# The key maximum over all partitions on TensorE instead of GpSimd, with GpSimd's scatters and two weight halves placed anew

## The reference, cut to what matters

```python
def softmax_kernel(data, proj, is_query, eps=0.0001):
    data_dash = jnp.einsum('bhnd,md->bhnm', data * normalizer, proj)
    diag = jnp.sum(data ** 2, axis=-1, keepdims=True) * 0.5 * normalizer ** 2
    if is_query:
        m = jnp.max(data_dash, axis=-1, keepdims=True)
    else:
        m = jnp.max(data_dash, axis=(-2, -1), keepdims=True)
    return ratio * (jnp.exp(data_dash - diag - m) + eps)
```

## Time and profile before

| | us |
|---|---|
| median of 3 runs | 1915.27 (1909.77 to 1923.55) |
| profiled execution, device time | 1906.49 |
| its span | 1904.7 |
| mean granted TensorE clock, share of full | 0.942 |

### The profile page before, as it was taken

The page is one execution under the profiler, slowest core; times in us unless marked ns, Lnnn a source line. Parts: engine busy times, 40 slices in busy tenths (PEclk is TensorE's granted clock), DMA queues, the critical chain, the costliest instruction groups (busy, mean ns, idle before and its releaser), DMA issues.

```text
span 1904.7 us, 19746 instructions
## 1 busy us (share of the span) xinstructions
PE 1707.0 (90%) x7679; PEld 1322.5 (69%) x7679; DVE 1101.8 (58%) x1835; ACT 673.7 (35%) x879; POOL 1000.7 (53%) x546
## 2 busy tenths in 40 slices
PE   6998999999896699999998299999999859999996
PEld 5664567788764456788886178787777747887863
DVE  7597758999875476756327433423433266623275
ACT  3323534332421244243331255655555412221112
POOL 3224561466778667548860456667676480152402
PEclk9999989999999688899999599999999979999988
DMA  8362111455332211122351767787777341121001
GB/s 331 95 207 50 1 1 48 122 111 111 62 78 22 23 1 1 23 67 45 66 160 34 260 204 264 250 275 246 247 270 240 136 122 45 45 89 43 24 1 45
DMA packets 146780, 212.56 MB, mean 112 GB/s; under 512 B 43740, under 2 KB 60352, under 8 KB 145440
## 3 DMA queue, kind: packets, MB, share of 16 engines
q1 hardware_dynamic: 98736, 177.49, 28.6%
q0 software_dynamic: 42832, 18.84, 8.3%
q10 hardware_dynamic: 5120, 14.99, 2.3%
HBM read 187.21 MB, written 30.08 MB: 114 GB/s over the span
## 4 chain that ended last, share of the span: by engine, by line
PE 65%; DVE 14%; POOL 6%; DMA 5%; ACT 5%; issue 4%; SPq 0%; POOLq 0%; DVEq 0%
PE PS L634 17%; PE PS L636 17%; PE PS L635 17%; PE PS L799 5%; PE PS L813 3%; DMA table_c<-edge_add,edge_ix 2%; POOL table_w L2293 2%; POOL table_c L2293 2%; PE PS L790 2%; ACT kd L1308 2%; PE PS L782 2%; DMA table_w<-edge_add,edge_ix 1%; POOL W L2218 1%; DVE h_op L1946 1%; POOL slots_x L2327 1%
## 5 line engine op out<-in xcount | busy, mean ns | idle before, releaser
L2218 POOL TENSOR_TENSOR W<-raw,W 128x2048 fp32r<-128x2048 f32 x40 | 192.4, 4813 | 330.8 <-ACT W L1158 323.6
L2293 POOL DMA_INDIRECT table_w<-edge_add,edge_ix x128 | 208.6, 1630 | 69.8 <-DMA table_w<-edge_add,edge_ix 39.7
L2293 POOL DMA_INDIRECT table_c<-edge_add,edge_ix x128 | 204.6, 1598 | 60.8 <-issue 33.5
L634 PE MATMUL PS<-op_b,W 128*128 128x512 f32 x576 | 225.5, 392 | 3.6 <-DVE op_b L2025 2.6
L635 PE MATMUL PS<-op_b,W 128*128 128x512 f32 x576 | 224.4, 390 | 0.0
L636 PE MATMUL PS<-op_b,W 128*128 128x512 f32 x576 | 224.4, 390 | 0.0
L634 PE MATMUL PS<-W,op_a 128*128 128x512 f32 x480 | 188.2, 392 | 2.9 <-DVE op_a L1755 1.8
L635 PE MATMUL PS<-W,op_a 128*128 128x512 f32 x480 | 187.1, 390 | 0.0
L636 PE MATMUL PS<-W,op_a 128*128 128x512 f32 x480 | 187.0, 390 | 0.0
L2332 POOL TENSOR_TENSOR W<-raw,W 128x2048 fp32r<-128x2048 f32 x30 | 143.5, 4792 | 56.4 <-ACT W L1389 56.4
L1158 ACT ACTIVATE W<-raw 128x2048 fp32r<-128x2048 f32 x40 | 76.5, 1920 | 158.6 <-PE PS L636 103.3
(11 more groups left out here) (419 smaller groups left out, 3824.2 us busy)
## 6 DMA issues: line engine op xcount, KB each, us to landing
raw<-in_L_ffn_w_dram SPq DMA_DIRECT2D x46, 1024.0 KB, 5.7
raw_e<-in_L_ffn_w_dram SPq DMA_DIRECT2D x22, 1024.0 KB, 5.9
raw_v<-in_L_ffn_w_dram SPq DMA_DIRECT2D x22, 1024.0 KB, 5.2
raw<-in_L_mix_W_dram SPq DMA_DIRECT2D x16, 1024.0 KB, 6.7
raw<-table_c SPq DMA_DIRECT2D x10, 1024.0 KB, 5.2
key_row<-key_dram SPq DMA_DIRECT2D x32, 256.0 KB, 4.0
w_row<-in_edge_weight_dram SPq DMA_DIRECT2D x32, 256.0 KB, 4.8
table_w<-zero POOLq DMA_DIRECT2D x4, 1024.0 KB, 7.9
```

The costliest lines, as they stand in the source:

```text
L634: pe.matmul(ps, lhs_hi, rhs_hi, start=start, stop=False)
L2218: pool.tensor_tensor(lo_at, raw[:, r % 2, :], hi_at.bitcast(F32), ALU.subtract).then_inc(lo_done, 1)
L2293: pool.indirect_dma_start(out=tb, out_offset=bass.IndirectOffsetOnAxis(ap=edge_ix[:, i, c:c + 1].bitcast(U32), axis=0), in_=edge_add[:, i, ...
```

## The change

The eight all-reduces on GpSimd go. TensorE turns `kmaxp` (128 x 2) into 2 x 128 by a transpose after the second query job (job `kt`), VectorE reduces it to `kneg` and multiplies a 2 x 2 unit matrix with it (`kdiag`), TensorE spreads it over 128 partitions by a product with ones after the fourth query job (job `kb`), and VectorE copies that to `nkmax`. ScalarE exponentiates two query tiles ahead of the keys. The column of ones in `V` is written once in place of eight times. GpSimd's scatters no longer stand between all-reduces: in layer 0, ten are put ahead of wo's low half and ten ahead of up's, and each of these two low halves waits for `kdiag_ready` of its pair; four more follow. In layer 1, 13 stand after wv, then wo, 12, up, 12 and 12. The totals (24 and 59 by the end of each attention part, with those of the query and key stage) stay the same.

```diff
--- before.py
+++ after.py
@@ -111,7 +111,8 @@
                    (f"v{l}", 1, "D"), (f"rk{l}", 2, "A"), (f"v{l}", 1, "D"), (f"dk{l}", 1, "A"), (f"v{l}", 6, "D"), (f"vsum{l}", 1, "A")]
         for hp in range(HEADS // 2):
             s = f"{l}.{hp}"
-            stages += [("kd" + s, 8, "AD"), ("qd" + s, 8, "A"), ("ctx" + s, 1, "D"), ("eT" + s, 8, "D"),
+            stages += [("kd" + s, 8, "AD"), ("qd" + s, 2, "A"), ("kt" + s, 1, "D"), ("qd" + s, 2, "A"),
+                       ("kb" + s, 1, "D"), ("qd" + s, 4, "A"), ("ctx" + s, 1, "D"), ("eT" + s, 8, "D"),
                        ("o" + s, 4, "D")]
         stages += [(f"wo{l}", 6, "D"), (f"y2_T{l}", 4, "AD"), (f"wo{l}", 2, "D"),
                    (f"up{l}.0", 2, "A"), (f"y2_T{l}", 4, "AD"), (f"up{l}.0", 6, "A"), (f"down{l}.0", 8, "D")]
@@ -332,7 +333,9 @@
         dexp = place("dexp", [P, 2, NT, HEADS])
         vsum = place("vsum", [P, HEADS, VW])
         kmax = place("kmax", [P, 2, NT])
-        kmaxp = place("kmaxp", [P, 2, 2])
+        kmaxp = place("kmaxp", [P, 2])
+        kneg = place("kneg", [2, 1])
+        kdiag = place("kdiag", [2, 2])
         nkmax = place("nkmax", [P, 2])
         nqmax = place("nqmax", [P, NT, 2])
         ctx_sb = place("ctx_sb", [P, 2, 4, DH])
@@ -439,8 +442,7 @@
         proj_loaded = sem("proj_loaded")
         vsum_ready = sem("vsum_ready")
         kmax_ready = sem("kmax_ready")
-        kmax_all = sem("kmax_all")
-        nkmax_ready = sem("nkmax_ready")
+        kdiag_ready = sem("kdiag_ready")
         kexp_done = sem("kexp_done")
         wg_ready = sem("wg_ready")
         chosen_ready = sem("chosen_ready")
@@ -777,10 +779,20 @@
                     s = f"{l}.{hp}"
                     for x, feat in (("kd", k_T), ("qd", q_T)):
                         for t in range(NT):
-                            n = JOB[x + s] + t
+                            n = JOB_AT[x + s, t]
                             open_job(n)
                             pe.matmul(bank(n), feat[:, hp, t * P:(t + 1) * P], proj[:, :, :].rearrange("p a m -> p (a m)"),
                                       start=True, stop=True).then_inc(job_full, 1)
+                            if x == "qd" and t == 1:
+                                n = JOB["kt" + s]
+                                open_job(n)
+                                pe.wait_ge(kmax_ready, 4 * l + hp + 1)
+                                pe.transpose(bank(n)[0:2, 0:P], kmaxp[:, :], ident[:, :]).then_inc(job_full, 1)
+                            if x == "qd" and t == 3:
+                                n = JOB["kb" + s]
+                                open_job(n)
+                                pe.wait_ge(kdiag_ready, 4 * l + hp + 1)
+                                pe.matmul(bank(n)[:, 0:2], ones[0:2, :], kdiag[:, :], start=True, stop=True).then_inc(job_full, 1)
 
                     def turn(t):
                         n = JOB_AT["eT" + s, t]
@@ -1297,16 +1309,18 @@
                             o_to_hi(hp - 1)
 
                     def query_exp(t):
-                        n = JOB["qd" + s] + t
+                        n = JOB_AT["qd" + s, t]
                         act.wait_ge(qbias_ready, NT * (4 * l + hp) + t + 1)
                         for h in range(2):
                             ins = act.activation(G[:, t, h * NBF:(h + 1) * NBF], bank(n)[:, h * NBF:(h + 1) * NBF], ACT.Exp, bias=nqmax[:, t, h:h + 1])
                         ins.then_inc(job_act, 1)
 
-                    act.wait_ge(nkmax_ready, 4 * l + hp + 1)
+                    for t in range(2):
+                        query_exp(t)
+                    act.wait_ge(job_done, DONES[JOB["kb" + s]])
                     for h in range(2):
                         act.activation(kd[:, h, :, :], kd[:, h, :, :], ACT.Exp, bias=nkmax[:, h:h + 1]).then_inc(kexp_done, 1)
-                    for t in range(NT):
+                    for t in range(2, NT):
                         query_exp(t)
                 o_to_hi(HEADS // 2 - 1)
                 split_hi(f"down{l}.0")
@@ -1669,6 +1683,7 @@
                     dve.wait_ge(job_full, n + 1)
                     if t == 0:
                         dve.wait_ge(job_act, ACTS[JOB[f"dk{l}"]])
+                        dve.tensor_copy(V[:, :, :, DH], dexp[:, 1, :, :])
                     link(dve.tensor_tensor(G[:, t, :], bank(n), rowv[:, row_at[f"bv{l}"] % 3, :], ALU.add))
                     if t:
                         ins = dve.tensor_tensor(v_sum[:, :], G[:, 0, :] if t == 1 else v_sum[:, :], G[:, t, :], ALU.add)
@@ -1677,8 +1692,7 @@
                         else:
                             ins.then_inc(vsum_ready, 1)
                     dve.tensor_tensor(V[:, t, :, 0:DH], G[:, t, :].rearrange("p (h d) -> p h d", h=HEADS),
-                                      dexp[:, 1, t, :].unsqueeze(2).to_broadcast([P, HEADS, DH]), ALU.mult)
-                    dve.tensor_copy(V[:, t, :, DH], dexp[:, 1, t, :]).then_inc(job_done, 1)
+                                      dexp[:, 1, t, :].unsqueeze(2).to_broadcast([P, HEADS, DH]), ALU.mult).then_inc(job_done, 1)
 
                 def o_to_lo(hp, c):
 
@@ -1697,16 +1711,23 @@
                         for c in range(2):
                             o_to_lo(hp - 1, c)
                     dve.wait_ge(job_done, DONES[JOB["kd" + s] + 7])
-                    dve.tensor_reduce(kmaxp[:, 0, :], kmax[:, :, :], AX_X, ALU.max).then_inc(kmax_ready, 1)
+                    dve.tensor_reduce(kmaxp[:, :], kmax[:, :, :], AX_X, ALU.max).then_inc(kmax_ready, 1)
                     for t in range(NT):
-                        n = JOB["qd" + s] + t
+                        n = JOB_AT["qd" + s, t]
                         dve.wait_ge(job_full, n + 1)
                         link(dve.tensor_reduce(nqmax[:, t, :], bank(n).rearrange("p (h m) -> p h m", h=2), AX_X, ALU.max,
                                                negate=True))
                         dve.tensor_tensor(nqmax[:, t, :], nqmax[:, t, :], dexp[:, 0, t, 2 * hp:2 * hp + 2], ALU.add).then_inc(qbias_ready, 1)
                         if t == 1:
-                            dve.wait_ge(kmax_all, 4 * l + hp + 1)
-                            dve.tensor_scalar(nkmax[:, :], kmaxp[:, 1, :], -1.0, None, ALU.mult).then_inc(nkmax_ready, 1)
+                            n = JOB["kt" + s]
+                            dve.wait_ge(job_full, n + 1)
+                            dve.tensor_reduce(kneg[:, :], bank(n)[0:2, 0:P], AX_X, ALU.max, negate=True).then_inc(job_done, 1)
+                            dve.wait_ge(job_done, DONES[n])
+                            dve.tensor_scalar(kdiag[:, :], ident[0:2, 0:2], kneg[:, :], None, ALU.mult).then_inc(kdiag_ready, 1)
+                        if t == 3:
+                            n = JOB["kb" + s]
+                            dve.wait_ge(job_full, n + 1)
+                            dve.tensor_copy(nkmax[:, :], bank(n)[:, 0:2]).then_inc(job_done, 1)
 
                     def e_t(t):
                         n = JOB_AT["eT" + s, t]
@@ -2295,16 +2316,19 @@
                     scattered[0] += 1
 
             for l in range(DEPTH):
-                for name in ("wq", "wk", "wv", "wo"):
+                for name in ("wq", "wk", "wv"):
                     if l == 0 or name != "wq":
                         lo(f"{name}{l}")
                     if l:
-                        scatter({"wq": 4, "wk": 6, "wv": 8, "wo": 5}[name])
-                lo(f"up{l}.0")
-                for hp in range(HEADS // 2):
-                    pool.wait_ge(kmax_ready, 4 * l + hp + 1)
-                    pool.partition_all_reduce(kmaxp[:, 1, :], kmaxp[:, 0, :], P, bass.bass_isa.ReduceOp.max).then_inc(kmax_all, 1)
-                    scatter(9 if l else 6)
+                        scatter({"wq": 4, "wk": 6, "wv": 13}[name])
+                for hp, name in enumerate((f"wo{l}", f"up{l}.0")):
+                    if l == 0:
+                        scatter(10)
+                        pool.wait_ge(kdiag_ready, hp + 1)
+                    lo(name)
+                    if l:
+                        scatter(12)
+                scatter(12 if l else 4)
                 lo(f"down{l}.0")
                 if l + 1 < DEPTH:
                     projection(l + 1)
```

## The result

The changed kernel takes 1840.11 us (median; 1839.12 to 1841.82) beside 1915.87 us (1909.77 to 1923.55) for the kernel before: ratio 0.9598, 95% interval 0.9563 to 0.9634. The forecast was 1843. The profiled execution has a span of 1838.9 us, 65.8 less than before; 72 were predicted.

What follows compares the result with a forecast made beforehand. TensorE, busy for 90% of the span, bounds the kernel; its waits and slow clock can be won. 6.2 + 2.25 + 3.4 + 29.7 + 34.9 - 4.5 = 72 us off 1904.7, plus 1.8 and 8.8: 1843 us, range 1832 to 1880.

Steps and rivals of the forecast that it cites:

- All-reduce out, pairs: Six ordinary head pairs: with kt and kb, each context starts 0.57 us earlier; 3.4 us, bounds +2 to -5.
- Pair 0 of layer 1: First context of layer 1 starts at 607.1 in place of 636.77, without the late all-reduce: 29.7 us.
- Clock: Contexts and the transposes behind them all run at full clock: 27.5 and 7.4 us, together 34.9 us.
- Low halves out of the value stage: Layer 0: value sum starts 6.2 us earlier without GpSimd's two subtractions, and sum to context gains 2.25 us more.
- Scatters of layer 0: They start at about 102, nothing on TensorE's path reads them; the tenth ends at 157, give or take 6.
- Rival B: Layer 0, pairs 0 and 1: low halves starting at kdiag block VectorE's small addition; 24.6 us, 1868 us, chance 0.26.
- Late low halves: Layer 1: up's and down's subtractions may hold up VectorE, each 0 to 4.6 us; 4.5 us taken for both.
- The way from span to median: Span 1832.7, with 1.8 us around it 1834.5; the median lies 8.8 us over the profiled execution: 1843 us.
- Rival C: Contexts load TensorE thinly, so their clock falls as before and 34.9 us are not won; 1878 us, chance 0.12.
- E: Layer 1: GpSimd's scatters delay down's low half, so TensorE waits before down; some 30 us go, 1873 us, chance 0.05.
- D: Every pair: TensorE-VectorE handshakes cost more than the all-reduce; slower from 1.6 us, at 4 us 1934 us; chance 0.03.

Runs made afterwards that it cites:

- e1: The changed kernel with wo's and up's low halves ahead of the pairs again, GpSimd's list ordered as in the kernel before; 1842.9 us, ratio 0.9601.
- e7: The changed kernel with each context also waiting for the third query tile's exponentials; 1910.36 us, ratio 0.9936.
- e3: The changed kernel without GpSimd's two waits on kdiag_ready in layer 0; 1842.29 us, ratio 0.963.
- e9: The kernel of e6 with two scatters fewer ahead of the low half of layer 1's wq and two more behind; 1839.59 us, ratio 0.9598.
- e4: The changed kernel with four scatters in place of ten ahead of wo's low half in layer 0, six more behind up's; 1861.53 us, ratio 0.9721.
- e5: The changed kernel with eight of layer 1's last twelve scatters moved behind down's low half; 1836.23 us, ratio 0.9587.
- e6: The kernel of e5 with up's low half of layer 1 also three scatters earlier; 1837.96 us, ratio 0.9591.
- e8: The changed kernel with the column of ones copied into V for each tile again, eight copies; 1841.58 us, ratio 0.9588.
- e2: The kernel before, all-reduce kept on GpSimd, with its low halves placed between the pairs' scatters as in the changed kernel; 1908.51 us, ratio 0.9943.
- e10: The kernel of e2 with two scatters between all-reduce and low half, the pair's other scatters behind the low half; 1901.56 us, ratio 0.9928.

## Why the prediction was right, and where only the sum was

- **All-reduce out, pairs.** Predicted 33.4 us from context to context and 0.57 us of gain in each; measured 33.46 to 33.54 in five of six and 35.65 in the one that the late low half of `up1.0` met; in layer 0, where the clock was full before too, the gain is 0.4 to 0.5 a pair. `kt` at 0.27 and `kb`'s two columns at 0.35 are nearly the 0.25 that I took. e1 shows this part of the change to bring 62 us, the new order of ScalarE's exponentials included.
- **Pair 0 of layer 1.** Predicted 29.7, measured 29.5, value sum to context.
- **Clock.** Predicted 34.9. L799 and L790 were 86.4 and 36.7 us in total, and the earlier trace rows together; L811 and L802 are 58.0 and 29.3: 35.8. e7 shows the cause.
- **Low halves out of the value stage.** The value sum came 8.05 us earlier, not 6.2; 1.6 of that lie in the products ahead of it (the key-head-rows job took 5.08 us before and 3.60 here and in e1, 5.26 and 5.29 in e3 and e9, with no edit near it), so the order's own share is 6.4. That share is steady: from the row products (L748) to the value sum it is 19.3 us in the changed kernel, e3, e4, e5, e6 and e9, and 25.8 before. The start of the value sum is not: 141.53 is the earliest of seven executions with the same code up to there, the latest 146.59 (e5). From sum to context I had 2.25 and got 0.4: the clock was 0.85 from 143 to 151. In e3, where it was 1.00, that stretch took 15.78 us, 1.8 less than before, nearly as the step had it; but e5, e6, e8 and e9 needed 17.2 to 17.5 as the changed kernel did. The step took the clock as full there, and it mostly was not.
- **Scatters of layer 0.** My estimate for the tenth was 157 plus or minus 6; it was 165.8. The error was on the harmless side. What set it was the one landing of 16.51 us. Rival B needed a tenth scatter before `kdiag` at 154.8, so it was 11 us from happening, and e4 shows what it would have cost.
- **Late low halves.** The term that was mis-sized: I took 4.5 us for both; they cost 2.1 and 7.2, and 9.3 in all. How much is luck of the meeting: with the same code there, e3 lost 1.4 and 5.5, and e8 nothing and 5.5. I had bounded each by the 4.6 us of the subtraction "and some clock", and left the clock out of the value. The place of the second was wrong too: I had it in the normalisation, and it met the splits behind it. A third, wq's, costs 5.3 in its stretch and about 3.3 by the value sum, but the stretch is as long in the kernel before (69.7 us).
- **The way from span to median.** I kept 10.6 us on top of the span from the kernel before. Here it is 1.2. The runs of kernels whose contexts sit at the edge of the clock scatter and those of the others don't: 1909.77 to 1923.55 before, 1890.56 to 1914.04 in e2, 1886.8 to 1917.64 in e7, and 1839.12 to 1841.82 after (4 runs before and after, 10 of e2 and e7). That the clock at the contexts makes the scatter I read from this; no run shows it by itself. The profiled execution of before, 1906.49, lay below all of those runs by such luck. So 1843.0 against 1840.11 is better than its parts: the span was forecast 6.2 us too short and the rest 9.4 us too long.
- **Rival C** (contexts slow whatever comes ahead) fell: all eight at 1.00. **E** did not come, TensorE waits for none of GpSimd's weights ahead of down. **D** is refuted by the pairs of 33.5 us.

## What to carry to other kernels

A wait of two microseconds ahead of a thin TensorE product can cost three times its length in the clock behind it (61.5 us for 18.0 in e7), so price such a wait by the slow stretch that follows it in the trace, not by its idle time. A GpSimd subtraction placed by counting scatters lands where the landings let it, and wq's met the two-operand work of VectorE in six of nine executions: place it by a wait on that work, or look in the trace for a stretch in which VectorE reads PSUM (neither was tried here). An all-reduce between GpSimd's tensor operations cost here far more than its own 0.37 us, since each change to it and from it took 6 to 8 us. And before moving an operation to another engine, ask whether the wait behind it ends by that operation at all, or by a bank that a reordering would free.

## What the runs showed of the hardware that I had not expected

- Each low half between two all-reduces had 6.8 to 7.7 us of "issue" ahead of it and each all-reduce behind a low half 5.9 to 8.5, scatters between them or not (e2, e10), but for one that waited 13.03 us for `kmaxp` anyway.
- 2.1 to 2.3 us of idle time ahead put all eight contexts of e7 at 0.51 to 0.59 of the clock; in the kernel before, 2.16 us ahead did so in some pairs and not in others. In e10, the fourth context of layer 0 ran at full clock (7.36 us) behind 2.16 us, and two of layer 1, behind 2.15 and 2.16, did not.
- A scatter of 128 elements waited 16.51 us for the landing of the one before while six large DRAM copies were under way.
- The time of a kernel with contexts at that edge varied by 14 to 31 us from run to run, that of the others by 3 to 10 (with fewer runs, 4 to 6).
